# Layer-1 block-sparse attention on eight cores: the global row in two halves of keys, and the scaling of probabilities shared between VectorE and GpSimd

## What is computed

```python
gq = qb[:, :, global_indices]
row_scores = jnp.einsum('bhgqd,bhkd->bhgqk', gq, k) * scale
out_rows = jnp.einsum('bhgqk,bhkd->bhgqd', jax.nn.softmax(row_scores, axis=-1), v)
kw = jnp.concatenate([jnp.roll(kb, 1, axis=2), kb, jnp.roll(kb, -1, axis=2)], axis=3)
local_scores = jnp.einsum('bhnqd,bhnkd->bhnqk', qb, kw) * scale
out_local = jnp.einsum('bhnqk,bhnkd->bhnqd', jax.nn.softmax(local_scores, axis=-1), vw)
col_scores = jnp.einsum('bhnqd,bhgd->bhnqg', qb, gk) * scale
out_gk = jnp.einsum('bhnqg,bhgd->bhnqd', jax.nn.softmax(col_scores, axis=-1), gv)
final = out_local + out_gk
final = final.at[:, :, global_indices].set(out_rows)
```

## Time and profile before

| what | value |
|---|---|
| median of 3 runs | 2205.42 us (2202.19 to 2438.12) |
| the profiled execution's own time | 2205.05 us |
| its span, slowest core (core 2) | 2203.5 us |
| spans of the eight cores | 2183.7 to 2203.5 us |
| TensorE busy | 1919.9 us, 87% of the span |
| VectorE busy | 1181.3 us, 54% |
| ScalarE busy | 1104.2 us, 50% |
| GpSimd busy | 92.9 us, 4% |

### The profile page before, as it was taken

How to read it: one execution, slowest core, us unless ns; L and a number is a source line. 1 busy time by engine, 2 the same in 40 slices (tenths; PEclk the granted TensorE clock), 3 DMA queues, 4 the chain that set the end, 5 groups by cost and what they waited for, 6 DMA issues and landing times. The chain is left out here.

```text
span 2203.5 us, 35508 instructions; the slowest of 8 cores (2183.7 to 2203.5 us)
## 1 busy us (share of the span) xinstructions
PE 1919.9 (87%) x12314; PEld 893.7 (41%) x12314; DVE 1181.3 (54%) x2093; ACT 1104.2 (50%) x2053; POOL 92.9 (4%) x151
## 2 busy tenths in 40 slices
PE   4899999987799995999988777777789899979999
PEld 2443333333344442444433444443334344434444
DVE  4334656455355421513635666666669588884442
ACT  5677777656311000111214667777768588873331
POOL 0000000000000000000000000000055100000000
PEclk9999999988899997999998888898889899989999
DMA  7204555200488506721001000100100422242331
GB/s 188 42 1 125 173 172 163 49 1 1 87 228 230 162 1 124 210 39 39 1 1 30 11 11 11 30 11 2 39 2 1 157 74 77 77 134 82 112 115 74
DMA packets 65180, 170.14 MB, mean 77 GB/s; under 512 B 4464, under 2 KB 37232, under 8 KB 57840
## 3 DMA queue, kind: packets, MB, share of 16 engines
q1 hardware_dynamic: 58496, 134.31, 18.8%
q0 software_dynamic: 6512, 33.56, 8.6%
HBM read 167.85 MB, written 33.55 MB: 91 GB/s over the span
## 5 line engine op out<-in xcount | busy, mean ns | idle before, releaser
L638 PE MATMUL f0R<-lnT,wgu 128*128 128x512 bf16 x1536 | 336.1, 382 | 25.6 <-DMA wgu<-f0wgu_d 25.6
L397 ACT ACTIVATE a0bq<-a0S 128x1024 bf16<-128x1024 f32 (+1 forms) x320 | 268.9, 893 | 119.3 <-PE a0S L317 118.2
L673 ACT ACTIVATE f0si<-f0R 128x1024 bf16<-128x1024 f32 x48 | 49.2, 1024 | 386.0 <-PE f0R L638 386.0
L638 PEld LDWEIGHTS f0R<-lnT,wgu 128*128 128x128 bf16 x1536 | 151.4, 99 | 210.0 <-issue 31.6
L1365 PE MATMUL g1hp<-q1T,t 128*128 128x512 bf16 x1024 | 226.3, 382 | 7.0 <-DVE g1a L1488 5.5
L1401 PE MATMUL g1hp<-g1t,q1T 128*128 128x512 fp8e4 x1024 | 223.0, 381 | 1.7 <-ACT q1T L1445 1.7
L699 DVE TENSOR_TENSOR f0hT<-f0si,f0R 128x1024 bf16<-128x1024 bf16 x48 | 58.6, 1222 | 224.7 <-PE f0R L638 224.7
L1121 ACT ACTIVATE a1pt<-a1T 128x768 bf16<-128x768 bf16 (+2 forms) x152 | 118.0, 783 | 84.2 <-PE a1T L1001 77.7
L934 PE MATMUL a1pj<-lnT,wqk 128*128 128x512 bf16 x512 | 151.0, 450 | 4.0 <-POOLq L880 4.0
L1365 PEld LDWEIGHTS g1hp<-q1T,t 128*128 128x128 fp8e4 x1024 | 98.9, 98 | 134.2 <-issue 22.0
L1401 PEld LDWEIGHTS g1hp<-g1t,q1T 128*128 128x128 bf16 x1024 | 100.5, 98 | 123.5 <-issue 4.1
(11 more groups left out here) (193 smaller groups left out, 2966.2 us busy)
## 6 DMA issues: line engine op xcount, KB each, us to landing
a0wst<-g1w_d SPq DMA_DIRECT2D x64, 512.0 KB, 4.7
f0wst<-g1w_d SPq DMA_DIRECT2D x32, 1024.0 KB, 6.7
hs_scr<-g1hsp SPq DMA_DIRECT2D x32, 512.0 KB, 3.3
q1T<-hs_scr SPq DMA_DIRECT2D x7, 2048.0 KB, 9.2
wgu<-f0wgu_d POOLq DMA_DIRECT2D x24, 512.0 KB, 7.4
xs<-x SPq DMA_DIRECT2D x8, 1024.0 KB, 12.7
t_scr<-f0wt SPq DMA_DIRECT2D x32, 256.0 KB, 2.6
xo<-xs SPq DMA_DIRECT2D x16, 512.0 KB, 9.1
```

The source lines that it names most:

```text
L397: s.activation(bq[:, u % 4, :, n0:512], sS[:, u % 2, :, n0:512], AF.Square).then_inc(s_sq, 1)
L638: mm = t.matmul(R[:, k % 4, 512 * n2:512 * (n2 + 1)], wgu[:, cc % 3, x, j, :], lnT[:, j, t0 + 512 * n2:t0 + 512 * (n2 + 1)], start=(j == 0 ...
```

## The change

The row is split into item 16 (keys 0 to 1023, two banks of `a1S`) and item 17 (keys 1024 to 2047, the other two banks). A pair has 18 items now. Each half has a maximum of its own, with which its exponentials are taken; at item 17 VectorE also takes the overall maximum, ScalarE computes the two factors exp(maximum of the half - overall maximum), and X of item 17 works out one scale for each half from the sums and the factors and scales the two halves. Everything behind it (three transpose groups and A) is as before, one step later. The waits on `a1S` become those of every other item: two items back. The projections are spread over 17 steps instead of 16.

In pairs 0 to 6 the scaling of the global keys' probabilities goes from VectorE to GpSimd (`s_p7` now counts GpSimd's share in all pairs), and T waits for both. GpSimd's weight loads are put at their places in the list, so that they stand between the scalings.

```diff
-    items = [(p, (m + 16) % 17) for p in range(8) for m in range(17)]
+    items = [(p, (m + 16) % 18) for p in range(8) for m in range(18)]
...
-        row = i >= 2 and i - 2 < len(items) and items[i - 2][1] == 16
-        if i >= 2 and i - 2 < len(items):
+        row = i >= 2 and i - 2 < len(items) and items[i - 2][1] == 17
+        if row:
+            out.append(("T", items[i - 2][0], 16, 0))
+        elif i >= 2 and i - 2 < len(items) and items[i - 2][1] < 16:
             out.append(("T",) + items[i - 2] + (0,))
...
-            due = (i % 17 * n + 15) // 16
+            due = (i % 18 * n + 16) // 17
...
                 for it in order:
+                    if it[0] == "P" and it[1] == "k" and it[3] == 3 and it[2] < 6:
+                        pr = it[2] + 2
+                        g.wait_ge(s_pj, signalled[it] + 1)
+                        g.dma_start(wqk[:, pr % 2, :, :, :],
+                                    wqk_d[pr, :, :, :, :]).then_inc(w_qk[pr % 2], 16)
...
+                    if it[0] == "X" and it[1] < 7 and it[2] < 16:
+                        _, pr, m = it
+                        g.wait_ge(s_rr, 16 * pr + m + 1)
+                        for u in range(1 if m == 0 else 0, 2):
+                            x = g.tensor_scalar(pp[:, m % 2, u, 256:384], pp[:, m % 2, u, 256:384],
+                                                rr[:, m % 2, 1, u:u + 1], None, ALU.mult)
+                        x.then_inc(s_p7, 1)
...
-                        if m == 0:
-                            t.wait_ge(s_x, item(pr, 0))
-                        else:
-                            t.wait_ge(s_x, item(pr, m) - 1)
+                        t.wait_ge(s_x, item(pr, m) - 1)
...
                         if pr >= 1:
-                            t.wait_ge(s_x, item(pr, 16))
-                        for c in range(4):
+                            t.wait_ge(s_x, item(pr, m) - 1)
+                        for c in range(2 * m - 32, 2 * m - 30):
...
-                        if pr == 7 and m < 16:
-                            t.wait_ge(s_p7, m + 1)
-                        else:
-                            t.wait_ge(s_p, item(pr, m) + 1)
+                        if m < 16:
+                            t.wait_ge(s_p7, 16 * pr + m + 1)
+                        if pr < 7 or m == 16:
+                            t.wait_ge(s_p, n_prob(pr, m))
...
-                        if pr >= 1:
+                        if pr >= 1 and m == 16:
                             s.wait_ge(s_T, use(pr - 1, 16, 2) + 1)
-                        s.activation(pr_[:, :], sR[:, :], AF.Exp, bias=nm[:, 2, 0, 0:1],
-                                     accum_out=den[:, 2, 0, 0:1]).then_inc(s_x, 1)
+                        x = m - 16
+                        if x == 1:
+                            s.activation(nm[:, 2, 1, :], nm[:, 2, 0, :], AF.Exp, scale=-1.0,
+                                         bias=rr[:, 2, 1, 0:1])
+                        s.activation(pr_[:, 1024 * x:1024 * (x + 1)], sR[:, 1024 * x:1024 * (x + 1)],
+                                     AF.Exp, bias=nm[:, 2, 0, x:x + 1],
+                                     accum_out=den[:, 2, 0, x:x + 1]).then_inc(s_x, 1)
...
-                            v.reciprocal(rr[:, m % 2, :, u0:2], den[:, m % 2, :, u0:2])
+                            v.reciprocal(rr[:, m % 2, :, u0:2], den[:, m % 2, :, u0:2]).then_inc(s_rr, 1)
...
-                                x = v.tensor_scalar(pp[:, m % 2, u, 256:384], pp[:, m % 2, u, 256:384],
-                                                    rr[:, m % 2, 1, u:u + 1], None, ALU.mult)
...
-                            v.reciprocal(rr[:, 2, 0, 0:1], den[:, 2, 0, 0:1])
+                            v.tensor_tensor(den[:, 2, 1, :], den[:, 2, 0, :], nm[:, 2, 1, :], ALU.mult)
                             v.drain()
-                            v.tensor_scalar(pr_[:, :], pr_[:, :], rr[:, 2, 0, 0:1], None,
-                                            ALU.mult).then_inc(s_p, 1)
+                            v.tensor_reduce(rr[:, 2, 1, 1:2], den[:, 2, 1, :], AX.X, ALU.add)
+                            v.drain()
+                            v.reciprocal(rr[:, 2, 1, 1:2], rr[:, 2, 1, 1:2])
+                            v.drain()
+                            v.tensor_scalar(rr[:, 2, 0, :], nm[:, 2, 1, :], rr[:, 2, 1, 1:2], None, ALU.mult)
```

More of the change, by code:

```diff
@@ L811, in item, with n_prob @@
     def item(pr, m):
-        return 17 * pr + (m + 1) % 17
+        return 18 * pr + (m + 2) % 18
+    def n_prob(pr, m):
+        return 17 * pr + (m + 1) % 17 + 1
     def use(pr, m, k=0):
@@ L880, in _ @@
                 g.drain().then_inc(cst, 1)
-                g.wait_ge(s_pj, n_pre)
-                g.dma_start(wv[:, :, :], wv_d[1, :, :, :]).then_inc(w_v, 16)
-                for pr in range(2, 8):
-                    g.wait_ge(s_pj, signalled[("P", "k", pr - 2, 3)] + 1)
-                    g.dma_start(wqk[:, pr % 2, :, :, :],
-                                wqk_d[pr, :, :, :, :]).then_inc(w_qk[pr % 2], 16)
-                g.wait_ge(s_pj, n_proj)
-                g.dma_start(wo[:, :, :], wo_d).then_inc(w_o, 16)
-                for it in order:
+                for it in order:
+                    if it[0] == "P" and it[1] == "k" and it[3] == 3 and it[2] < 6:
[3 more added lines that the diff above has]
+                                    wqk_d[pr, :, :, :, :]).then_inc(w_qk[pr % 2], 16)
+                    if it == ("P", "k", 7, 3):
+                        g.wait_ge(s_pj, n_proj)
+                        g.dma_start(wo[:, :, :], wo_d).then_inc(w_o, 16)
+                    if it[0] == "P" and it == ("P", "v", 0, NT - 1):
+                        g.wait_ge(s_pj, n_pre)
+                        g.dma_start(wv[:, :, :], wv_d[1, :, :, :]).then_inc(w_v, 16)
+                    if it[0] == "X" and it[1] < 7 and it[2] < 16:
[5 more added lines that the diff above has]
+                        x.then_inc(s_p7, 1)
                     if it[0] == "X" and it[1] == 7 and it[2] < 16:
                         m = it[2]
-                        g.wait_ge(s_rr, m + 1)
+                        g.wait_ge(s_rr, 16 * 7 + m + 1)
                         for u in range(1 if m == 0 else 0, 2):
@@ L1181, in _ @@
                         v.wait_ge(s_S, item(pr, m) + 1)
-                        v.tensor_reduce(nm[:, 2, 0, 0:1], sR[:, :], AX.X, ALU.max,
-                                        negate=True).then_inc(s_mx, 1)
+                        x = m - 16
+                        mx = v.tensor_reduce(nm[:, 2, 0, x:x + 1], sR[:, 1024 * x:1024 * (x + 1)], AX.X,
+                                             ALU.max, negate=True)
+                        if x == 1:
+                            v.drain()
+                            mx = v.tensor_tensor(rr[:, 2, 1, 0:1], nm[:, 2, 0, 0:1], nm[:, 2, 0, 1:2],
+                                                 ALU.min)
+                        mx.then_inc(s_mx, 1)
                     elif it[0] == "X" and it[1] == 7 and it[2] < 16:
@@ L1187, in _ @@
                         if m >= 2:
-                            v.wait_ge(s_p7, m - 1)
+                            v.wait_ge(s_p7, 16 * 7 + m - 1)
                         u0 = 1 if m == 0 else 0
                         v.reciprocal(rr[:, m % 2, :, u0:2], den[:, m % 2, :, u0:2]).then_inc(s_rr, 1)
-                    elif it[0] == "X":
+                    elif it[0] == "X" and it[2] != 16:
                         _, pr, m = it
@@ L1199, in _ @@
                                 lo = 64 if u == 0 else 0
-                                v.tensor_scalar(pp[:, m % 2, u, lo:lo + 192],
-                                                pp[:, m % 2, u, lo:lo + 192],
-                                                rr[:, m % 2, 0, u:u + 1], None, ALU.mult)
-                                x = v.tensor_scalar(pp[:, m % 2, u, 256:384], pp[:, m % 2, u, 256:384],
-                                                    rr[:, m % 2, 1, u:u + 1], None, ALU.mult)
+                                x = v.tensor_scalar(pp[:, m % 2, u, lo:lo + 192],
+                                                    pp[:, m % 2, u, lo:lo + 192],
+                                                    rr[:, m % 2, 0, u:u + 1], None, ALU.mult)
                             x.then_inc(s_p, 1)
                         else:
-                            v.reciprocal(rr[:, 2, 0, 0:1], den[:, 2, 0, 0:1])
+                            v.tensor_tensor(den[:, 2, 1, :], den[:, 2, 0, :], nm[:, 2, 1, :], ALU.mult)
                             v.drain()
-                            v.tensor_scalar(pr_[:, :], pr_[:, :], rr[:, 2, 0, 0:1], None,
-                                            ALU.mult).then_inc(s_p, 1)
+                            v.tensor_reduce(rr[:, 2, 1, 1:2], den[:, 2, 1, :], AX.X, ALU.add)
+                            v.drain()
+                            v.reciprocal(rr[:, 2, 1, 1:2], rr[:, 2, 1, 1:2])
+                            v.drain()
```

(7 more changed lines are left out.)

17 lines of the change are left out of this document (9 added, 8 removed).

## The result

The changed kernel takes 2247.37 us (median of 4 runs, lowest 2244.5). The kernel before took 2203.86 us on the same chip. The ratio is 1.019, with a 95% interval of 1.0173 to 1.0207: slower by 43.5 us. The forecast was 2198 us with a range of 2176 to 2228. The direction was wrong, and the range missed it. Some executions of most kernels here ran slower, at a lower granted clock on half of the cores or on all; they are in the medians but not in the ratios, so the lowest time stands beside a median that they lift.

The account below looks back on a forecast made before the run. Waits, not a full engine, were taken to bound the stage. Pairs 0 to 3 gain 7.6 us, pairs 4 to 6 lose 2, pair 7 gains 2: 7.6 us off 2205.05, predicting 2198 us, range 2176 to 2228.

Parts of the forecast that it names:

- the row in two halves: Row of pairs 0 to 6: S no longer waits for the row's and item 15's exponentials; 14.9 us gained.
- GpSimd's half of X: Scaling of global keys in pairs 0 to 6: T starts 1.68 us behind the reciprocal instead of 1.43.
- In a step without P this costs 0.25 us: Each step without a projection, pairs 0 to 6: T's later release costs 0.25 us, bounds 0 and 1.05.
- at the row: Clock charge in the row's stretch, pairs 0 to 3: one and a half of three projections at half clock, 2.5 us.
- hidden, with no margin behind k and v: Steps with a projection: GpSimd's scaling ends at 3.06 to 3.4 us, T stands at 2.97 + 0.40, so no cost.
- The working of the stretch: S of item 15 to S of item 2, worked in pair 2 at full clock: 17.4 us, was 22.82.
- the working without the charge for the clock: The row's gains in pairs 0 to 6 at full clock, with no projections counted as slowed by half clock.
- In pair 7, 2 us of gain: Pair 7: S of the row no longer waits and its halves overlap; about 2 us gained, 0 to 4.
- Rival 2: T behind GpSimd: VectorE stretches one GpSimd scaling by 0.40 us in every item; 2236 us, chance 0.17.
- Rival 1: Pairs 0 to 6: the clock stays up and no projection of the new stretches loses time; 2179 us, chance 0.15.
- Rival 3: Row's transposes and A: gain given back waiting for X of item 17 and ScalarE; 2205 us, chance 0.18.
- a double step of 5.6: Sign in the profile after: one step with a projection and one without together take 5.6 us.
- The last line of the forecast: Wrong if GpSimd's scaling is well above 0.60, P steps exceed 3.0, L1226 shows 0.8 us, or clock leaves 0.83 to 0.95.

Follow-up runs that it names:

- run 1: Changed kernel with VectorE doing both scalings of pairs 0 to 6 again, so the row in two halves alone: 2207.06 us, 1.000 against the kernel before.
- Run 4: Changed kernel plus six overwritten 128x512 matmuls ahead of T in each item after a step without a projection: 2206.32 us, 1.0006 against the kernel before.
- run 5: Row in two halves with VectorE's scaling, plus five overwritten matmuls before T after each step without a projection: 2178.14 us, 0.9879 against the kernel before.
- run 11: run 5 with overwritten matmuls also in pair 7 and at each row's second transpose group and A: 2167.59 us, 0.9839 against the kernel before.
- run 3: Changed kernel with GpSimd scaling only block u=1 and VectorE the other block: 2203.09 us, 0.999 against the kernel before.
- run 9: run 1 plus three extra VectorE scalings into an unused tile ahead of the real ones: two lowest times 2255.5 and 2258.0 us, 2203.15 before.
- run 10: run 1 plus one extra VectorE scaling ahead of the real ones: ratio 1.0078 against the kernel before, lowest 2218.91 us.

## Why the prediction was wrong

The forecast for pairs 0 to 6 was 7.6 - 2 = 5.6 us shorter; it became 39.2 longer. The forecast splits in two parts that run 1 measures apart, and both parts missed.

```
pairs 0 to 6, us                  forecast    measured
the row in two halves              -14.9        -5.5    (run 1 less before)
GpSimd's half of X                  +9.3       +44.7    (after less run 1)
sum                                 -5.6       +39.2
```

The 9.3 are the forecast's own 0.25 us in 4 steps of four pairs and 7 of three; the 14.9 is what is left.

**The step that failed: "GpSimd's half of X", "In a step without P this costs 0.25 us".** Two things were wrong in it.

- The size. The number of steps was right, 4 x 4 + 3 x 7 = 37. The chain was 0.33 + 1.20 + 0.14 = 1.68. It measured 0.33 + 1.24 + 0.36 = 1.93. I took the 0.14 from VectorE's end to T and gave it to GpSimd. None of the rows that I had chosen showed a TensorE instruction released by GpSimd, but the trace of the kernel before has one, in pair 7:

```profile
1606.07 0.61 POOL L897 TENSOR_SCALAR a1pp<-a1pp,a1rr 128x128 bf16<-128x128 bf16 x1
...
1606.93 0.80 PE L1001 MATMUL a1T<-ident,a1pp 128*128 128x128 bf16 x6 [3.06 <-POOL a1pp L897]
```

It shows 0.25 (1606.68 to 1606.93), nearly twice the 0.14, and still less than the 0.36 of pairs 0 to 6. So the way out wanted bounds of its own and not VectorE's value. With what it measured the term is 0.50, 37 times: 18.5 us in place of 9.3. The measured shortest double step confirms it (5.87 for 5.37 in run 1).
- The kind. I worked out the step at full clock, and priced the clock only "at the row". But the wait that grew stands in front of a projection in every step without P. It grew from 1.4 us on the mean (30 waits) to 1.8 (48 waits), and half of the projections outside the row's stretches took 2.8 to 3.6 us instead of 1.90 (27 of 54; 11 in run 1). Over the 37 double steps the mean grew by 1.10 us and the shortest by 0.50, so 0.60 x 37 = 22 us is clock; without the row's own it is 0.71 x 34 = 24. Run 4 gives the other view of it: 42.5 us come back when only the wait is filled and nothing is released earlier. It also fills waits that the changed kernel shares with run 1, so it is above the 22; runs 4 and 5, both filled, leave 26.0 for the late release and thus 18.7 of the 44.7 for the clock. 19 to 24 us is what I can state.

The P steps that I called "hidden, with no margin behind k and v" added a little: a P step behind a P step takes 3.07 on the mean (20 of them) where run 1 has 2.99.

**The row.** This term missed too, 5.5 us gained for 14.9. The stage in four parts, as the mean of the eight cores; a stretch is from S of item 15 to S of item 2 (in pair 0 from S of the row), and the forecast is that for the row alone, with what it charged for the clock.

```
us                                  before   forecast   run 1   run 11
stretches at the row, pairs 0 to 3    85.5       76.3    77.6     66.5
stretches at the row, pairs 4 to 6    60.1       58.3    65.6     58.9
the other steps, pairs 0 to 3        153.4      151.0   155.6    147.9
the other steps, pairs 4 to 6        112.4      110.6   108.1    102.8
```

The working of the stretch held where it was worked through, in pairs 0 to 3. At full clock it gave 19.2 less for the four, 66.3, and run 11, with the clock at 1.00, has 66.5. It did not hold in pairs 4 to 6, to which it was carried over: there the stretch should have become 1.8 us shorter in all and became 5.5 longer, the largest part of the miss. TensorE in pair 5 of run 1:

```profile
1468.76 0.27 PE L959 MATMUL a1S<-a1kT,a1qT 64*64 64x192 bf16 x2
...
1470.78 0.50 PE L1009 MATMUL a1T<-ident,a1pp 128*128 128x128 bf16 x6 [1.55 <-DVE a1yT L1246]
...
1471.50 0.62 PE L989 MATMUL a1S<-a1kT,a1qT 64*64 64x512 bf16 x4
...
1476.48 3.08 PE L944 MATMUL a1pj<-lnT,wqk 128*128 128x512 bf16 x8
...
1482.54 1.44 PE L1015 MATMUL a1T<-ident,a1pr 128*128 128x128 bf16 x12 [2.03 <-DVE a1yT L1246]
...
1487.56 3.57 PE L944 MATMUL a1pj<-lnT,wqk 128*128 128x512 bf16 x8
1491.06 0.37 PE L959 MATMUL a1S<-a1kT,a1qT 64*64 64x192 bf16 x2
```

With eight projections a pair the step of item 15 follows one without P, T in it waits 1.55 us, and S of item 16 comes 2.74 behind S of item 15 in pairs 5 and 6, in place of the 1.15 worked out for pair 2. T of the row waits another 2.03. And both projections of the stretch are at the lower clock for most of their time, in each of the three pairs, where one was slow before and one more was charged. Even at a clock of 0.97 to 1.00, in run 11, the stretch is 19.6 us a pair and not 17.5. In the other steps of pairs 0 to 3 the gain of 2.4 became a loss of 2.2, with 8 slow projections for 4.

Run 5, where the clock holds at 0.94 to 0.95, has 29.3 us less than before, and the working without the charge for the clock gives 30.3. That they agree is luck: in run 5 the stretches give 13.2 for 26.1, and the other steps, in which the fillers work, 15.2 for 4.2. In pair 7, 2 us of gain were forecast, and the part behind its row got 2.5 us longer in run 1 and 1.3 in the changed kernel.

**The rivals.** Rival 2 named the place, T behind GpSimd, and its 2236 us is nearest to the result; that is luck. Its mechanism is not what the runs show. It wanted GpSimd's scaling stretched by 0.40 us. The groups of the changed kernel:

```profile
L904 POOL TENSOR_SCALAR a1pp<-a1pp,a1rr 128x128 bf16<-128x128 bf16 x217 | 135.2, 632 | 305.7 <-DVE a1rr L1222 305.7
...
L1226 DVE TENSOR_SCALAR a1pp<-a1pp,a1rr 128x192 bf16<-128x192 bf16 x217 | 60.8, 321 | 10.7
```

GpSimd's takes 0.63 with VectorE at work beside it and 0.60 alone; the two VectorE scalings take 0.56 together, and end long before GpSimd does. Run 3 keeps the overlap and loses nothing, and run 9 has the loss without GpSimd. The lock in the Trainium skill, SBUF — State Buffer, section "SBUF: two separate sides", would have one of the two wait for the whole of the other, where VectorE's is in a two-port mode. This trace shows no such wait: the two engines' scalings overlap in every item, and cost each other 0.03 and 0.05 us on the mean, 0.06 and 0.11 in run 3. Whether VectorE's were in such a mode no run shows. Rival 1 (the clock stays up) is the reverse of what happened; that its 2179 us are near the 2178 of run 5 is luck too, for the reason given above, and run 5 has nothing of GpSimd's. Rival 3 is close to run 1, 2205 and 2207 us, but the gain was lost in the stretches of pairs 4 to 6 and in the clock: in pair 3 of the changed kernel T of the row came at 11.35 for 10.65, and the small steps of X cost no more than that.

**The signs that I had named.** Named and seen: S not waiting for the row's exponential (but twice, 1.3 us), T waiting for L904 (in 48 steps for "some 40"), GpSimd at 0.60 (0.63). Named and broken: periods of 58.5 and 58 (64.4 and 65.9), a double step of 5.6 (7.54 in the median), P steps of no more than 3.0 (3.07), and the clock below 0.83 in pair 4. The last line of the forecast said that this would make it wrong; but no case in it had a price for it, and so the range ended at 2228.

## What to carry to other kernels

Work that is moved to another engine is paid for by the chain to whoever waits for it, hand-over in and hand-over out with that engine's own numbers, and the freed engine's slack is worth nothing when it was not last; moving half as much (run 3) stayed under the chain that was there. A wait of TensorE that grew by half a microsecond in a loop was paid twice here, once as time and once by the clock of the matmuls behind it, so price both, and multiply it by the steps of the whole loop, not only where the change is. And where TensorE's clock falls in waits, two changes can be worth nothing apart and something together: the split row alone gave 1.000, matmuls that nothing reads alone gave 1.0012, both together 0.9879, and 0.984 with more places filled (2167.6 against 2203 us). So a change that shortens waits is to be tried with the clock held up too, before it is dropped.

## What the runs showed of the hardware that I had not expected

- From GpSimd's last instruction to the TensorE instruction that it releases: 0.35 to 0.36 us in 43 of 48 cases in pairs 0 to 6 of the changed kernel, and 0.25 in the one case of pair 7 before, where VectorE's end to T is 0.14.
- T released 0.50 us later: 27 of 54 projections took 2.8 to 3.6 us in place of 1.90, for 11 of 54 in run 1, and the granted clock of pair 4 was 0.79, for 0.86 in run 1. No wait of TensorE in pairs 0 to 6 was longer than 2.51 us. Delays of 0.18 and 0.51 us lengthened the stage by 15.3 and 54.1 us (runs 10 and 9, against run 1).
- TensorE was granted 1.00 over 215.52 us when its waits were filled with 128x512 matmuls (run 11), for 0.89 over 237.89 us without (run 1): more work on the engine, and 5.6 us less for each of pairs 0 to 3.
- A GpSimd and a VectorE scaling that run side by side in every item slow each other by 0.03 and about 0.05 us on the mean (VectorE's 128x192 0.32 for 0.27); in run 3 GpSimd's takes 0.66 for 0.60 and VectorE's 128x128 0.36 for 0.25.
